# A third group gathered into the staging area, and a rearranged end, in a graph-network kernel on one core

## The reference

```python
h = relu(layernorm(x))                                   # 12500 x 256
messages = concat([h[src], edge_attr], -1) @ W_message   # 212500 x 256
agg = segment_sum(messages, dst)
u = layernorm(relu(agg) + h) * scale1 + bias1
u = u + relu(u @ W0 + b0)
u = u + relu(u @ W1 + b1)
w = u + u @ W2 + b2
out = x + layernorm(h + w) * scale2 + bias2
```

## Time and profile before

| | us |
|---|---|
| median of 3 executions | 2111.95 (2110.2 to 2114.55) |
| the profiled execution | 2110.9 |
| its span in the trace | 2109.0 |
| TensorE's matrix instructions busy | 1622.2 (77%) |
| GpSimd busy | 1566.3 (74%) |
| VectorE busy | 967.0 (46%) |
| ScalarE busy | 408.2 (19%) |

### The profile page before, as it was taken

How to read it: one execution, slowest core, us unless ns; L and a number is a source line. 1 busy time by engine, 2 the same in 40 slices (tenths; PEclk the granted TensorE clock), 3 DMA queues, 4 the chain that set the end, 5 groups by cost and what they waited for, 6 DMA issues and landing times.

```text
span 2109.0 us, 40441 instructions
## 1 busy us (share of the span) xinstructions
PE 1622.2 (77%) x6722; PEld 1119.1 (53%) x6723; DVE 967.0 (46%) x4164; ACT 408.2 (19%) x1209; POOL 1566.3 (74%) x1637
## 2 busy tenths in 40 slices
PE   0089967788778788888877788777878787878886
PEld 0057745565556555555555555445555554645554
DVE  8975534344344444343434344334434334434345
ACT  6852111111111111111111111111111111111112
POOL 7757777777777777777777777777777777777773
PEclk9999988899889899899899999989999999898999
DMA  9996655566556665565656556556555556655551
GB/s 386 348 201 169 174 160 161 160 168 167 155 161 166 166 165 159 157 168 159 161 161 166 158 162 166 155 158 167 150 161 160 162 153 165 165 155 160 153 174 57
DMA packets 372316, 359.43 MB, mean 170 GB/s; under 512 B 258336, under 2 KB 315744, under 8 KB 371968
## 3 DMA queue, kind: packets, MB, share of 16 engines
q0 software_dynamic: 78192, 213.62, 35.9%
q1 hardware_dynamic: 237184, 90.49, 16.9%
q10 hardware_dynamic: 56592, 51.54, 7.8%
HBM read 328.99 MB, written 26.48 MB: 169 GB/s over the span
## 4 chain that ended last, share of the span: by engine, by line
POOL 70%; issue 23%; PE 4%; DMA 1%; DVE 1%; ACT 0%; POOLq 0%; DVEq 0%; ACTq 0%
POOL ring L459 69%; PE acc_banks L657 1%; DMA ring<-h_table,src_all 1%; POOL xs L471 1%; PE agg_bank L528 1%; PE agg_bank L533 0%; PE y_bank L516 0%; PE z_bank L516 0%; DMA xs<-x,src_all 0%; PE acc_banks L665 0%; POOLq L1243 0%; ACT ring L790 0%; DVE onehot L1210 0%; PE st_bank L539 0%; PE z_bank L522 0%
## 5 line engine op out<-in xcount | busy, mean ns | idle before, releaser
L459 POOL DMA_INDIRECT ring<-h_table,src_all x1549 | 1484.1, 958 | 484.4 <-issue 470.2
L657 PE MATMUL acc_banks<-ring,onehot 128*128 128x320 f32 x3290 | 1048.4, 469 | 303.7 <-DMA ring<-h_table,src_all 210.5
L657 PEld LDWEIGHTS acc_banks<-ring,onehot 128*128 128x128 f32 x3290 | 639.4, 203 | 673.2 <-issue 489.1
L1210 DVE TENSOR_SCALAR onehot<-iota,dst_rel 128x128 f32<-128x128 f32 x1664 | 349.7, 297 | 297.1 <-PE acc_banks L657 271.7
L860 DVE TENSOR_TENSOR visit_rows<-agg_bank,visit_rows 128x256 f32<-128x256 f32 x98 | 41.6, 425 | 769.4 <-PE agg_bank L533 763.4
L707 ACT ACTIVATE uT<-z_bank,fp 128x128 f32<-128x128 f32 x196 | 78.9, 453 | 1265.6 <-PE z_bank L522 1265.6
L528 PE MATMUL agg_bank<-wm,ST 128*128 128x256 f32 (+1 forms) x582 | 169.6, 414 | 0.0
L528 PEld LDWEIGHTS agg_bank<-wm,ST 128*128 128x128 f32 (+1 forms) x582 | 109.0, 200 | 58.6 <-issue 38.7
L713 ACT ACTIVATE r_bank<-y_bank,fp 128x128 f32<-128x128 f32 x196 | 58.6, 338 | 292.0 <-PE y_bank L516 284.9
L533 PE MATMUL agg_bank<-wl,u 128*128 128x256 f32 x392 | 112.6, 410 | 0.0
L516 PEld LDWEIGHTS y_bank<-u,wl 128*128 128x128 f32 x784 | 104.7, 194 | 5.6 <-issue 0.3
(11 more groups left out here) (175 smaller groups left out, 1151.6 us busy)
## 6 DMA issues: line engine op xcount, KB each, us to landing
ring<-h_table SPq DMA_DIRECT2D x4096, 1.0 KB
ring<-edges SPq DMA_DIRECT2D x206, 256.0 KB
ring<-h_table,src_all POOLq DMA_INDIRECT x1549, 3.2
h_in<-h_table ACTq DMA_DIRECT2D x98, 128.0 KB
visit_rows<-h_table ACTq DMA_DIRECT2D x98, 128.0 KB
visit_rows<-x ACTq DMA_DIRECT2D x98, 128.0 KB
out<-o ACTq DMA_DIRECT2D x93, 128.0 KB
xs<-x SPq DMA_DIRECT2D x10, 896.0 KB, 14.1
```

The lines of the kernel that those rows point to most:

```text
L459: nc.gpsimd.indirect_dma_start(out=ring[:, k * G + j, 0:D], out_offset=None, in_=rows, in_offset=bass.IndirectOffsetOnAxis(ap=src_all[:, g ...
L657: return nc.tensor.matmul(acc_of(at), onehot[:, hot + j, :], rhs[:, slot * G + j, :], start=False, stop=True, skip_group_check=True)
L1210: op = nc.vector.tensor_scalar(onehot[:, ((k + AHEAD) % OG) * G + j, :], iota[:, :], dst_rel[:, bass.ds((g + AHEAD) * G + j, 1)], None, AL ...
```

## The change

Three parts. First, `EG` becomes 3: a third group, group 10, lies in the staging area. It is gathered from the table, not from `x` (`RAW_EG` stays 2, so 10 groups are still gathered from `x`), and GpSimd doesn't wait for a slot of the ring ahead of it. The ring's groups begin with group 11 (`FIRST`), and the tail has 5 groups in place of 6.

Second, the room that this takes is where addresses were. Only the addresses of the first 12 tiles (`EARLY`, three rounds of the loop) are copied ahead; after the third round SyncE waits for the staging area to be read, and copies the other 20 into it. The tiles that SyncE fetches are the same as before.

Third, the end. In a group of the tail that closes a block, TensorE makes the visit after three tiles (`SPLIT`) instead of seven, and the close and the transposes of the new sums when the seventh tile is added (`pe_split_visit`). On VectorE the branch on `passes` stands ahead of the last visit.

```diff
-EG = 2
+EG = 3
+RAW_EG = 2
+SPLIT = 3
...
-    RAWS = RG + EG
+    RAWS = RG + RAW_EG
+    FIRST = RG + EG
...
-            for n in range(SP_TILES):
-                sp.dma_start(rows_flat[:, n * P:(n + 1) * P], src_bytes[:, n:n + 1],
-                             allow_slow_non_contiguous=True).then_inc(row_src_in, 16)
-            sp.wait_ge(row_src_in, 16 * SP_TILES)
+            def copy_addresses(table, first, count):
+                for n in range(count):
+                    sp.dma_start(table[:, n * P:(n + 1) * P], src_bytes[:, first + n:first + n + 1],
+                                 allow_slow_non_contiguous=True).then_inc(row_src_in, 16)
+                sp.wait_ge(row_src_in, 16 * (first + count))
+
+            copy_addresses(early_rows, 0, EARLY * len(SP_AT))
...
-                load_edges(h % RG, o * LOOP + RAWS + h, o * LOOP + RG + h + EG + 1)
+                g = o * LOOP + FIRST + h
+                load_edges(h % RG, g, g + 1)
...
+            for h in range(SP_FIRST + 1):
+                load_edges(h, FIRST + h, RG + h + 1)
+            with nc.Fori(0, EARLY, engines=[mybir.EngineType.SP], hint_back_edge=True) as o:
+                three_rounds(o, early_rows, o * len(SP_AT))
+            sp.wait_ge(group_free, RG + FIRST)
+            copy_addresses(late_rows, EARLY * len(SP_AT), (LOOPS - EARLY) * len(SP_AT))
+            with nc.Fori(EARLY, LOOPS, engines=[mybir.EngineType.SP], hint_back_edge=True) as o:
+                three_rounds(o, late_rows, o * len(SP_AT) - EARLY * len(SP_AT))
...
+            for g in range(RAWS, FIRST):
+                for j in range(G):
+                    nc.gpsimd.indirect_dma_start(
+                        out=extra[:, (g - RG) * G + j, 0:D], out_offset=None, in_=h_table,
+                        in_offset=bass.IndirectOffsetOnAxis(ap=src_all[:, g, j:j + 1], axis=0),
+                    ).then_inc(extra_in[j // PT], 16)
+            for g in range(FIRST, NG):
+                k = (g - FIRST) % RG
+                pool.wait_ge(group_free, g + 1 - (EG if g < FIRST + RG else 0))
...
+        def pe_split_visit(pe, n, sel, tiles, close):
+            pe.wait_ge(z_ready, n + 1)
+            transposed(z, zT).then_inc(zT_done, 1)
+            pe.wait_ge(ST_ready, n + 1)
+            aggregated(ST, agg).then_inc(agg_ready, 1)
+            last_layer(u2, back).then_inc(back_ready, 1)
+            layer_matmuls(1, u1, y[1]).then_inc(y_ready[1], 1)
+            pe.wait_ge(u_in, n + 1)
+            layer_matmuls(0, uT, y[0]).then_inc(y_ready[0], 1)
+            tiles()
+            close()
+            pe.wait_ge(block_saved, n + 1)
+            sums_transposed().then_inc(st_done, 1)
+            open_acc(sel)
...
+                if fetched == "tail":
+                    for j in range(SPLIT):
+                        rows_of(j)
+                        tile(j)
+                    with nc.tensor.If(closes > 0):
+                        pe_split_visit(pe, visit, steered[VSEL], lambda: up_to_last(SPLIT), close)
+                    with nc.tensor.Else():
+                        up_to_last(SPLIT)
...
-            dve_visit(dve, nc.s_assert_within(tail + 0, 0, NB - 1))
-            with nc.vector.If(passes < 2):
-                dve_end(dve)
-            with nc.vector.Else():
+            with nc.vector.If(passes > 1):
                 with nc.vector.Fori(1, passes) as p:
...
-                    dve_visit(dve, nc.s_assert_within(p + tail, 0, NB - 1))
-                dve_end(dve)
+                nc.vector.nop()
+            dve_visit(dve, NB - 1)
+            dve_end(dve)
```

More of the change, by code:

```diff
@@ L283, in build @@
         edges_in = [sem(f"edges_in{k}") for k in range(RG)]
+        extra_in = [sem(f"extra_in{q}") for q in range(PAIRS)]
         extra_edges_in = [sem(f"extra_edges_in{e}") for e in range(EG)]
@@ L485, in _ @@
                 gather(k, k, x, [raw_in[k]] * PAIRS)
-            for e in range(EG):
+            for e in range(RAW_EG):
                 gather_extra(e)
@@ L607, in group @@
             def group(p, i, k, fetched, tiles=G):
-                offset = {"raw": 0, "extra": RG, "middle": RAWS, "tail": RAWS + MID * RG, "later": 0}[fetched]
+                offset = {"raw": 0, "extra": RG, "middle": FIRST, "tail": FIRST + MID * RG, "later": 0}[fetched]
                 g = i * (LOOP if fetched == "middle" else RG) + k + offset
```

74 lines of the change are left out of this document (42 added, 32 removed).

## The result

The changed kernel takes 2099.34 us (median of 4 executions, 2098.11 to 2101.23), the kernel before 2113.05 beside it (4 executions). The ratio is 0.9934, with an interval of 0.9921 to 0.9947. The forecast was 2095.7 in a range of 2093 to 2103. The profiled execution took 2098.11, with a span of 2096.7, where it was 2109.0 before.

The account below looks back on a forecast made before the run. GpSimd's gathers, 1549 at 1.26 us, were taken to bound the kernel. Gains of 10.1 + 0 + 4.3 + 1.9 = 16.3 us took the profiled 2110.9 to 2094.6; with the median 1.05 above, 2095.7, range 2093 to 2103.

Parts of the forecast that it names:

- The sum of 16.3 us: Forecast gain over the whole kernel: 10.1 + 0 + 4.3 + 1.9 us.
- the prediction's own signs: Wrong if GpSimd waits for TensorE at 200-400 or 850-950 us, group 2 ends after 141, or releaser-less pauses follow the last gather.
- Part one: Third staged group at the start: GpSimd leaves the gate 8 gathers further on, last gather issued 10.1 us earlier.
- the gate of group 2: GpSimd's wait for TensorE to finish group 2, at 140.84 us; claimed unchanged, met at the 25th gather instead of the 17th.
- Part two: Late address copies by SyncE after the third round: a 16 us stop plus some 3 us landing, covered by room, worth 0.
- Part three: Split visit in TensorE's tail: the end's first product at 2079.6 instead of 2083.93 us, 4.3 us earlier.
- Part four: VectorE's branch moved ahead of its last visit: the 2.02 us pause in its end goes, gaining 1.9 us.
- The 7 us of cover: VectorE's idle time from 2066 to 2073.0 us ahead of its last visit, claimed to hide the jump's cost of 2 to 6 us.
- Fetching at the end: Rival, 0.18: VectorE's 2.0 us pause stays or moves, or one up to 6.0 us comes on TensorE; 2097.7 to 2101.7 us.
- The lead lost in part: Rival, 0.13: traffic delays group 2, or TensorE behind SyncE's rows holds GpSimd; 3 to 10.1 us lost, 2098.7 to 2105.8.
- The late addresses: Rival, 0.03: SyncE's copying stops the core beyond the 39 us room; at 5 us a copy, 45 us slower, 2157 us.
- the start did what it says: Opposes a rival, 0.06: group 10 issued no earlier or the gate not group 2's, only the end faster; 2105.8 to 2107.7 us.

Follow-up runs that it names:

- the split alone: The kernel before with only the split visit and its branch in TensorE's tail: 2117.04 us, ratio 0.9992; on the slow chip 3480.98 us, ratio 0.9995.
- the start alone: The changed kernel's staging area and late addresses, with TensorE's tail and VectorE's branch as before: 2100.59 us, ratio 0.9951; on the slow chip 3511.77 us, ratio 1.0118.
- three copies: The changed kernel with SyncE copying the 20 late addresses three times, each time with a wait for their landing: 2115.67 us, ratio 0.998.
- lighter visits: The changed kernel with products left out of TensorE's first two visits, in groups 2 and 4: 2094.55 us, ratio 0.9928; on the slow chip 3490.29 us, ratio 1.0036.
- other senders: The changed kernel with senders of real edges, not node 0, in the last tiles' unused places: 2105.89 us; with the visit after two tiles too, 2100.28 us.
- 24 sums: The changed kernel with 14 more VectorE sums of two SBUF operands just ahead of its ten before the last visit: 2108.91 us, ratio 0.9958.

## Why the prediction was right, and where its terms were off

Each part did what was forecast of it, and the time is in the range. The sum of 16.3 us was 12.3 in the profiled span, and 2099.34 lies above the forecast's own range of 2093.5 to 2098.5, in the part that was there for the rivals. By the prediction's own signs it is not clean either. A wait of GpSimd for TensorE appeared between 200 and 400 us (1.31 us at 203.14), group 2 was done later than 141, and TensorE had a pause of 0.97 us without a releaser behind the last gather's issue. The three were small; each had been named as showing the prediction wrong.

**Part one, 10.1 us, measured 6.7.** The step that was mis-sized is that the 25th gather passes the same gate at the same time, and that nothing stands behind it. The eight gathers are 10.0 us. Of these are lost:

- 1.3 us at the gate of group 2, at 142.16 and not 140.84. The reason is in VectorE's row: it waited for the last group from `x`, and its first `z`, which TensorE's first visit needs, was written at 135.07, and at 133.75 before. The timeline of VectorE in the changed kernel:

```profile
115.71 0.43 DVE L1138 BATCH_NORM_STATS2 x_stats<-xs 128x6 f32<-128x256 f32 x1 [2.17 <-DMA xs<-x,src_all]
...
135.07 0.41 DVE L954 TENSOR_SCALAR z<-visit_rows,mv,rstd 128x256 f32<-128x256 f32 x1
```

  and in the kernel before:

```profile
114.08 0.43 DVE L1078 BATCH_NORM_STATS2 x_stats<-xs 128x6 f32<-128x256 f32 x1 [0.86 <-DMA xs<-x,src_all]
...
133.75 0.41 DVE L894 TENSOR_SCALAR z<-visit_rows,mv,rstd 128x256 f32<-128x256 f32 x1
```

  The last gather from `x` took 2.34 us here and 0.94 before. This goes with the execution, not with the change: it was 2.34 in the split alone, whose start is that of before, and 0.94 in the start alone. With 0.94 the changed start met the gate at 141.06 (three copies) and 141.18 (start alone), before at 140.84; with 2.34 at 142.14 to 143.38 (five profiles), before's start at 141.56 (one). So 0.2 to 0.3 us, or 0.6 to 1.8, may be the traffic that the prediction put at 0 with 3.7 as its end; with one profile of before's start in each case this stays an estimate.

- 1.3 us up to a second gate, which the prediction did not see. The 72nd gather opens group 19 and waits for group 11. From the gate of group 2 TensorE works off a backlog without a pause, and has group 11 done 60.98 us after that gate, in seven profiles of the changed start to 0.01 us. GpSimd's 47 gathers took 59.66 us before (140.84 to 200.50), 1.32 less: 1.01 us are its wait beyond the usual 0.30, the rest slower gathers. Before, the gather that needs group 11 came eight gathers later, at 210.56, and found it done. TensorE's row of before already had it: its first 18 of 32 instructions finish group 11, at about 201.5, where the prediction's own 140.84 + 47 x 1.26 is 200.1.

```profile
196.54 8.78 PE L657 MATMUL acc_banks<-ring,onehot 128*128 128x320 f32 x32
```

  The prediction looked for the tightest place behind SyncE's tiles, at group 29; it should have gone through every group from the first gate on. The lighter visits removed both gates.

- 0.7 us in the gathers behind it, which is less than executions differ by: from the 72nd gather to the last it was 1863.4 to 1875.0 us in the ten profiles on ordinary chips (1865.3 in the kernel before, 1866.0 in the changed one). The estimate of 1.26 us a gather stood.

**Part two, 0: right.** The stop was 20.6 us (forecast 16 and a landing of some 3), TensorE waited 34.33 us at its end, and GpSimd did not. The room behind it was 23.5 us, forecast 20. Copied three times, it cost GpSimd 7.0 us.

**Part three, 4.3 us, measured 3.5.** The visit lies where it was forecast, and z, written at 2070.94, is 2.8 us early. Two things were off. The first is what was replaced: the prediction took the old visit's 6.8 us as it stood, but in that execution the granted clock was 0.57 in the visit's first 3 us, and at the full clock it is 1.3 us shorter. Against an execution at the full clock the term is 2.1 us; 3.5 holds only against the one that the prediction had read. The second was the landing of the last pair, taken from a usual one as 2.94 us: it was 3.79, in part since most of the last tile's senders are one node. The prediction also took it for granted that the data would be the bound. In three profiles of the changed end (5.17, 5.37 and 5.38 us behind the last gather) TensorE's own 13.1 to 13.2 us from the visit's start were. The data are the bound, and the product 4.56 to 4.70 us behind the gather, only where a gather stands still in between, or where the visit begins a pair earlier.

**Part four, 1.9 us, measured 2.1: right in size.** With the branch ahead of the visit, and the visit's code shorter, the pause was absent in all nine profiles, on either chip, and present in all five without, at 1.9 to 2.05 us. (The end part was 22.9 to 23.0 us in eight of the nine and 24.5 with three copies, where the pause was absent too and the span ended 1.5 us later behind the last store's issue.) That it is the engine waiting for its own instructions fits, and was not shown by itself. The rule of the Trainium skill that the prediction weighed ("Runtime: NRT & Kernel Launch", section "Instruction fetch mechanics") says that a taken branch out of the held pages stalls. No row shows such a stall between the sums and the visit, and it did not lie under a wait of VectorE, as the prediction had it. The 7 us of cover were gone, since the visit's operands came earlier too: VectorE waited 0.16 us in the changed kernel, and not at all with the visit after two tiles and other senders, where the visit's first instruction starts 0.34 us behind the last sum, as one sum behind another, with the branch between them:

```profile
2063.23 0.42 DVE L1281 TENSOR_TENSOR xs<-xs,rows 128x256 f32<-128x256 f32 x1
2063.57 0.42 DVE L920 TENSOR_TENSOR visit_rows<-agg_bank,visit_rows 128x256 f32<-128x256 f32 x1
```

Whether a fetch ran beside the ten sums was not tested. With 24 sums there is a pause of 1.34 us without a releaser, one instruction into the visit:

```profile
2073.11 0.42 DVE L923 SCALAR_TENSOR_TENSOR visit_rows<-agg_bank,h_in 128x256 f32<-128x256 f32 x1 [1.34 <-issue]
```

TensorE's own work was the bound there, so it cost nothing that shows.

**The rivals.** Fetching at the end: no pause behind the last gather but one of 0.9 to 1.2 us of TensorE ahead of the last group's tiles, which every kernel with the split visit has and the start alone has not; what of it costs is in the 3.5 us. The lead lost in part: this is what happened, 3.4 us of 10.1, within the 3 to 10.1 us that this rival gave. Group 2 was later, as it said, and TensorE held GpSimd, but at group 11 and not behind SyncE's rows. The late addresses cost 0, and the start did what it says.

The fastest kernel was the one with lighter first visits, 2094.55 us. It leaves out products on which no output depends for these inputs only, and half of its lead over the changed kernel's last gather is the gather that stood still.

## What to carry to other kernels

When a producer is moved forward by n steps, go through every later hand-over in order, not only the ones that look tight before: a consumer that works off a backlog without a pause has a fixed pace (60.98 us for nine groups with visits here), and the producer's own pace decides at which of them it arrives first. Where only the last arrival counts, look at what that transfer holds, padding included, and take its landing from its own row. When a stretch of before is taken as a price, look at the granted clock in it first: from the same visit's start to the end's product it was 8.9 us at the full clock and 10.2 in the profile that was read. And when work is put ahead of the last data, compare its length with the time to them: 13.1 us of work begun 7.8 us ahead of a gather ends later than the data do.

## What the runs showed that was not expected

**A gather that stands still beside VectorE's sums, or doesn't.** VectorE's ten sums of two operands in SBUF, back to back, last 3.36 us. In the changed kernel the gather that starts beside them lasts 3.42 us, with the first of the sums ahead of it:

```profile
2058.37 0.42 DVE L1280 TENSOR_TENSOR xs<-xs,rows 128x256 f32<-128x256 f32 x1
...
2059.21 3.42 POOL L478 DMA_INDIRECT ring<-h_table,src_all  x1 [0.30 <-issue]
```

In the kernel before it is one of 3.83 us. In all six profiles with such a gather it ends 4.25 us behind the first sum, whenever it began (0.42 to 1.01 us behind it). In the four others on ordinary chips every gather beside the sums passes in at most 1.16 us. With the lighter visits a gather started 0.87 us behind the first sum, where the changed kernel's started 0.84 behind:

```profile
2054.14 0.41 DVE L1281 TENSOR_TENSOR xs<-xs,rows 128x256 f32<-128x256 f32 x1
...
2055.01 1.03 POOL L478 DMA_INDIRECT ring<-h_table,src_all  x1 [0.30 <-issue]
```

So it is all or nothing, and a few hundredths of a microsecond may decide; beside a burst of 24 no gather was held. The Trainium skill ("SBUF — State Buffer", section "Who interferes with whom") says that a VectorE instruction with two inputs in SBUF contends with a GpSimd instruction that reads SBUF. A gather reads its indices there, and the traces agree in that each held gather ends only 0.8 us behind the last sum's end. It does not explain the four profiles in which none is held. Why a gather is held over all ten instructions in some executions and over none in others stays open. It costs 2.3 to 2.9 us, more than one of this change's parts.

**TensorE's clock near the end** was at 0.50, the 1.2 GHz level, for a stretch of some 3 to 7 us in several profiles, at different places: ahead of the visit in the changed kernel, up to 2 or 3 us into the visit in the kernel before, and with other senders in most of it. In that last run TensorE needed 16.4 us from the visit's start to the end's product, where it was 13.1 to 13.2 at the full clock. What made the clock fall at one place or the other was not tested.
